# Context times Wo added to x as a step of its own, and a third key tile added on VectorE, in a fused attention, decoder and expert kernel

## The reference, cut to what matters

```
h   = x + relu(x @ w_down) @ w_up                 # w_down, w_up made from the condition
sim = cumulative products of path agreements      # from sigmoid(h @ Wp + bp), 8 heads, depth 5
ctx = softmax(causal sim) @ (h @ Wv)              # 8 heads of 32 numbers
x   = x + ctx @ Wo
U   = cond @ W_dec + b_dec                        # per batch: 257 rows of 30
z   = x @ U[:-1] + U[-1]                          # 30 numbers a token
y   = z @ V                                       # the decoder's output, 256 numbers
e   = argmax over 8 experts of y @ gate_w.T
out = x + y + y @ expert_w[e].T
```

## Time and profile before

| | |
|---|---|
| executions shown | 152.51, 152.74, 153.7 us; median 152.74 us |
| profiled execution | 153.3 us, of which the span is 151.2 us |
| TensorE (PE) busy | 141.7 us, 94% of the span |
| VectorE (DVE) busy | 87.6 us, 58% |
| ScalarE (ACT) busy | 56.4 us, 37% |
| GpSimd (POOL) busy | 30.2 us, 20% |
| chain of work that ended last | TensorE 84%, VectorE 11% |
| granted TensorE clock | 1.000 of full speed |

### The profile page before, as it was taken

How to read it: one execution, slowest core, us unless ns; L and a number is a source line. 1 busy time by engine, 2 the same in 40 slices (tenths; PEclk the granted TensorE clock), 3 DMA queues, 4 the chain that set the end, 5 groups by cost and what they waited for, 6 DMA issues and landing times.

```text
span 151.2 us, 5082 instructions
## 1 busy us (share of the span) xinstructions
PE 141.7 (94%) x2294; PEld 89.3 (59%) x2294; DVE 87.6 (58%) x164; ACT 56.4 (37%) x67; POOL 30.2 (20%) x56
## 2 busy tenths in 40 slices
PE   5999679999979979999999999999999999999993
PEld 5646346554645655657566756576567677666651
DVE  0473727866794848387816575549256852975431
ACT  3013370564253225357522461673234447310010
POOL 7200022011042120650112224200222440110000
PEclk9999999999999999999999999999999999999999
DMA  4999999700111000000000000000011010101111
GB/s 109 316 399 424 385 365 351 255 9 0 18 32 21 4 0 4 0 4 4 35 35 4 35 7 4 35 4 32 3 39 39 0 38 1 39 35 39 69 41 69
DMA packets 7381, 12.50 MB, mean 83 GB/s; under 512 B 1552, under 2 KB 5808, under 8 KB 7232
## 3 DMA queue, kind: packets, MB, share of 16 engines
q1 hardware_dynamic: 7120, 11.73, 21.9%
q0 software_dynamic: 96, 0.05, 0.9%
q10 hardware_dynamic: 144, 0.39, 0.6%
HBM read 9.95 MB, written 2.22 MB: 81 GB/s over the span
## 4 chain that ended last, share of the span: by engine, by line
PE 84%; DVE 11%; issue 2%; ACT 1%; POOL 0%; POOLq 0%; ACTq 0%; DVEq 0%
PE work L588 39%; PE c_ps L588 23%; PE s_ps L588 16%; PE work L767 3%; DVE rden L440 2%; PE work L707 2%; DVE h_t L473 1%; ACT prob L387 1%; DVE feat L578 1%; DVE u_w L514 1%; DVE phi_t L490 1%; PE work L759 1%; DVE w_up L466 1%; DVE x_t L566 1%; DVE q_bd L495 0%
## 5 line engine op out<-in xcount | busy, mean ns | idle before, releaser
L387 ACT ACTIVATE prob<-s_ps 128x1536 f32<-128x1536 f32 (+1 forms) x24 | 38.3, 1594 | 43.5 <-PE s_ps L588 43.4
L440 DVE RECIPROCAL rden<-c_ps 128x256 f32<-128x256 f32 x16 | 28.1, 1758 | 22.7 <-PE c_ps L588 22.7
L364 POOL TENSOR_SCALAR_AFFINE_SELECT prob<-prob 128x1024 f32<-128x1024 f32 x16 | 19.2, 1202 | 90.3 <-ACT prob L387 90.3
L588 PE MATMUL s_ps<-phi_t 32*128 32x256 f32 (+1 forms) x384 | 24.2, 365 | 1.1 <-DVE phi_t L490 0.6
L588 PE MATMUL c_ps<-prob,v_sb 128*32 128x256 f32 (+1 forms) x384 | 24.9, 346 | 0.0
L588 PEld LDWEIGHTS s_ps<-phi_t 32*128 32x128 f32 x384 | 17.4, 184 | 11.1 <-issue 8.5
L588 PE MATMUL work<-ctx_t,mix_sb 128*32 128x256 f32 x256 | 17.0, 381 | 0.4
L588 PE MATMUL work<-zo_t,gexp 128*32 128x256 f32 x256 | 16.9, 379 | 0.0
L588 PEld LDWEIGHTS c_ps<-prob,v_sb 128*32 128x32 f32 x384 | 11.6, 110 | 8.7 <-issue 1.7
L588 PE MATMUL c_ps<-prob,ones 128*32 128x256 f32 (+1 forms) x256 | 16.3, 326 | 0.0
L588 PE MATMUL work<-w_vl,h_t 128*32 128x296 f32 x208 | 14.8, 416 | 0.9 <-DVE pick L551 0.5
(11 more groups left out here) (96 smaller groups left out, 133.3 us busy)
## 6 DMA issues: line engine op xcount, KB each, us to landing
wdec<-in_W_dec SPq DMA_DIRECT2D x1, 3855.0 KB, 18.2
x_t<-in_x_tr SPq DMA_DIRECT2D x4, 512.0 KB, 8.7
ex_t<-in_expert_tr SPq DMA_DIRECT2D x1, 2048.0 KB, 25.2
out_x<-x_t SPq DMA_DIRECT2D x16, 128.0 KB, 1.7
mix_sb<-in_mix SPq DMA_DIRECT2D x1, 776.0 KB, 19.7
lift_sb<-in_lift ACTq DMA_DIRECT2D x1, 384.0 KB, 3.8
w_vl<-in_vl SPq DMA_DIRECT2D x1, 296.0 KB, 5.0
first_sb<-in_first SPq DMA_DIRECT2D x1, 144.0 KB, 3.4
```

The source lines that it names most:

```text
L364: nc.gpsimd.affine_select(out=tri, in_=tri, compare_op=ALU.is_ge, fill=0.0, base=0, pattern=[[0, HG], [0, 2], [1, P]], channel_multiplier= ...
L387: nc.scalar.activation(prob[:, p % 2, :, 0:width(p)], s_ps[:, :, 0:width(p)], ACT.Exp).then_inc(exped, 1)
L440: link(nc.vector.reciprocal(rden[:], c_ps[m % 2][:, CW:2 * CW]))
L588: return nc.tensor.matmul(o, w, r, start=start, stop=stop, skip_group_check=True)
```

## The change

There is a new step `mix`, four to a batch: context times Wo alone (8 matmuls where `out` had 16), which VectorE adds to x in place. `out` keeps the half with the expert's matrix, and VectorE adds that as before, so that 16 such additions become 32. `zT` waits for the four (in the last batch: two and two) `mix` steps and uses the new x alone, with half its matmuls; `WoU` and its copy are gone, and so is the transposed Wo in the load of the weights.

In the last pair of a long chunk, VectorE now adds key tile 2 into `tiles` as well, after the exponential and the mask; the ones of that tile go from TensorE, and the ones times `tiles` come last in the pair's matmuls. This holds for 7 of the 8 long chunks; the last pair of the kernel is left as it was. `add` thus stands ahead of 15 pairs instead of 8.

`zs` copies the scores to SBUF and releases its bank with that copy; the search for the best expert reads the copy, and a new count (`picked`) tells GpSimd of its end.

```diff
+def long(p):
+
+    return pair(p)[1][1] == 1 and p < ALL - 1
+
+
 def adds(p):
 
-    return sum(opening(i) for i in range(p + 1))
+    return sum(long(i) for i in range(p + 1))
...
-    elif n1 < B:
-        gaps[0] += [("WoU",)] if b == 1 else []
-        gaps[1] += [("zs", prv, ALL_T), ("zo", prv, 0), ("zo", prv, 1), ("VL", n1, 0), ("VL", n1, 1)]
-        gaps[2] += [("VL", n1, 2), ("VL", n1, 3)]
     else:
-        gaps[1] += [("zs", prv, ALL_T), ("zo", prv, 0), ("zo", prv, 1)]
-        gaps[4] += [("zs", b, FIRST), ("zo", b, 0)]
-    if prv >= 0:
-        gaps[3] += [("zoT", prv, 0), ("zoT", prv, 1)]
+        gaps[1] += [("mix", prv, 3)]
+        gaps[3] += [("zs", prv, ALL_T), ("zo", prv, 0), ("zo", prv, 1)]
+        gaps[4] = [("zoT", prv, 0), ("zoT", prv, 1)] + gaps[4]
+        if n1 < B:
+            gaps[1] += [("VL", n1, 0)]
+            gaps[2] += [("VL", n1, 2)]
+        else:
+            gaps[5] += [("zs", b, FIRST), ("zo", b, 0)]
...
-        gaps[3] += [("Q",), ("gup", n2)]
-        gaps[4] += [("G", 0), ("ubT",)]
+        gaps[3] += [("Q",), ("gup", n2), ("mix", b, 0)]
+        gaps[4] += [("G", 0), ("ubT",), ("mix", b, 1)]
         gaps[5] += [("G", 1), ("down", n2)]
     else:
-        gaps[0] += [("zT", prv, ALL_T)]
-        gaps[3] += [("out", prv, 0)]
-        gaps[4] += [("out", prv, 1)]
-        gaps[5] += [("out", prv, 2)]
+        gaps[0] += [("mix", prv, 2)]
+        gaps[2] += [("zT", prv, ALL_T)]
+        gaps[3] += [("mix", b, 0)]
+        gaps[4] += [("out", prv, 0), ("mix", b, 1)]
+        gaps[5] += [("out", prv, 1)]
+        if n2 < B:
+            gaps[5] += [("down", n2)]
+    if prv >= 1:
+        gaps[0] += [("out", prv - 1, 2)]
+        gaps[1] += [("out", prv - 1, 3)]
     if b >= 1 and n1 < B:
-        gaps[2] += features(n1, ALL_T)
-    if prv >= 1:
-        gaps[1] += [("out", prv - 1, 3)]
-    if b >= 1 and n2 < B:
-        gaps[5] += [("down", n2)]
+        gaps[1] += [("VL", n1, 1)]
+        gaps[2] += [("VL", n1, 3), *features(n1, ALL_T)]
     if b == B - 1:
-        gaps[2] += [("zT", b, FIRST)]
-        gaps[5] = [("zoT", b, 0), ("out", prv, 2), ("out", prv, 3)]
+        gaps[3] = [("mix", b, 0)]
+        gaps[4] = [("mix", b, 1), ("out", prv, 0), ("zT", b, FIRST)]
+        gaps[5] = [("out", prv, 1), ("zoT", b, 0), ("out", prv, 2)]
...
-        if _p + 1 < ALL and opening(_p + 1):
+        if _p + 1 < ALL and long(_p + 1):
             ORDER += [("add", _p + 1)]
-ORDER += [("zT", B - 1, SECOND), ("out", B - 1, 0), ("zs", B - 1, SECOND), ("zo", B - 1, 1),
-          ("out", B - 1, 1), ("zoT", B - 1, 1), ("out", B - 1, 2), ("out", B - 1, 3)]
...
+                    acc = tiles[:, chunk(p) % 2]
                     dve.wait_ge(exped, p + 1)
-                    nc.vector.tensor_tensor(tiles[:, chunk(p) % 2], both[:, :, 0, :], both[:, :, 1, :], ALU.add
-                                            ).then_inc(added, 1)
+                    if opening(p):
+                        nc.vector.tensor_tensor(acc, both[:, :, 0, :], both[:, :, 1, :], ALU.add).then_inc(added, 1)
+                    else:
+                        dve.wait_ge(masked, masks(p))
+                        dve.wait_ge(added, adds(p) - 1)
+                        nc.vector.tensor_tensor(acc, acc, both[:, :, 0, :], ALU.add).then_inc(added, 1)
...
+                    sc = score[:, span]
...
+                    nc.vector.tensor_copy(sc.rearrange("p t e -> p (t e)"), bank(s)[:, P:P + nt * E]
+                                          ).then_inc(empty(s), 1)
+                    done(dve, s)
                     link(nc.vector.reduce_max(smax[:, span], sc, AX_X))
...
-                if half and last:
-                    pe.wait_ge(added, adds(p))
-                    for h in range(HG):
-
-                        mm(c_ps[m % 2][DH * h:DH * (h + 1), CW:2 * CW], ones[:], tiles[:, m % 2, h, :],
-                           start=False, stop=False)
                 for i, (kt, q0, n) in enumerate(units):
                     lo = q0 % CW
                     for h in range(HG):
                         ins = mm(c_ps[m % 2][DH * h:DH * (h + 1), lo:lo + n],
                                  v_sb[:, b % 2, kt, DH * (HG * g + h):DH * (HG * g + h + 1)],
                                  prob[:, p % 2, h, CW * i:CW * i + n], start=(kt == 0), stop=(last and i == 1))
-                    if half and first:
+                    if half and (first or i == 0 and p < ALL - 1):
                         continue
                     for h in range(HG):
 
                         ins = mm(c_ps[m % 2][DH * h:DH * (h + 1), CW + lo:CW + lo + n], ones[:],
-                                 prob[:, p % 2, h, CW * i:CW * i + n], start=False, stop=(last and i == 1))
+                                 prob[:, p % 2, h, CW * i:CW * i + n], start=False, stop=(not half and i == 1))
+                if half and last:
+                    pe.wait_ge(added, adds(p))
+                    for h in range(HG):
+
+                        ins = mm(c_ps[m % 2][DH * h:DH * (h + 1), CW:2 * CW], ones[:], tiles[:, m % 2, h, :],
+                                 start=False, stop=True)
                 ins.then_inc(summed, 1)
...
-                elif kind == "WoU":
...
-                        done(pe, ("WoU",))
-                    pe.wait_ge(ctx_ready, BC * b + (NG if ts == FIRST else BC))
-                    for c in range(2 * DC):
+                        pe.wait_ge(u_ready, 1)
+                    for i in range(TT):
+                        if i // DC in (t // 2 for t in ts):
+                            done(pe, ("mix", b, i))
+                    for c in range(DC):
                         for t in ts:
-                            tok = slice(P * t, P * (t + 1))
-                            w = u_w[:, c, b, :] if c < DC else wo_u[:, c - DC, KP * b:KP * (b + 1)]
-                            r = x_t[:, b, c, tok] if c < DC else ctx_t[:, b % 2, c - DC, tok]
-                            ins = mm(o[KP * t:KP * (t + 1), 0:P], w, r, start=(c == 0), stop=(c == 2 * DC - 1))
+                            ins = mm(o[KP * t:KP * (t + 1), 0:P], u_w[:, c, b, :], x_t[:, b, c, P * t:P * (t + 1)],
+                                     start=(c == 0), stop=(c == DC - 1))
...
-                elif kind == "out":
+                elif kind in ("mix", "out"):
                     _, b, i = s
-                    if b == 0 and i == 0:
-                        done(pe, ("G", 0))
-                        done(pe, ("G", 1))
                     row, half = slice(P * (i % DC), P * (i % DC + 1)), slice(CW * (i // DC), CW * (i // DC + 1))
-                    for c in range(2 * DC):
-                        if c == DC:
-                            done(pe, ("zoT", b, i // DC))
-                        w = wo[:, c, row] if c < DC else gexp[:, c - DC, row]
-                        r = ctx_t[:, b % 2, c, half] if c < DC else zo_t[:, c - DC, half]
-                        ins = tiled(o[:, 0:CW], w, r, start=(c == 0), stop=(c == 2 * DC - 1))
+                    if kind == "mix":
+                        if b == 0 and i == 0:
+                            pe.wait_ge(ld_mix, 16)
+                        pe.wait_ge(ctx_ready, BC * b + NG * (i // DC + 1))
+                    else:
+                        if b == 0 and i == 0:
+                            done(pe, ("G", 0))
+                            done(pe, ("G", 1))
+                        done(pe, ("zoT", b, i // DC))
+                    for c in range(DC):
+                        w = wo[:, c, row] if kind == "mix" else gexp[:, c, row]
+                        r = ctx_t[:, b % 2, c, half] if kind == "mix" else zo_t[:, c, half]
+                        ins = tiled(o[:, 0:CW], w, r, start=(c == 0), stop=(c == DC - 1))
```

More of the change, by code:

```diff
@@ L247, in build @@
         kmax = sb("kmax", [P, TT])
+        score = sb("score", [P, TT, E])
         hit = sb("hit", [P, TT, E])
@@ L282, in build @@
         u_ready = sem("u_ready")
+        picked = sem("picked")
         zo_ready = sem("zo_ready")
@@ L806 @@
         "vl": halves(np.concatenate([a["attn_Wv"], a["attn_Wp"]], axis=1)),
-        "mix": np.concatenate([halves(a["attn_Wo"]), halves(a["attn_Wo"].T), v4, halves(v4.T),
+        "mix": np.concatenate([halves(a["attn_Wo"]), v4, halves(v4.T),
                                halves(a["ffn_gate_w"].T)], axis=1),
```

32 lines of the change are left out of this document (11 added, 21 removed).

## The result

| | before | after |
|---|---|---|
| executions, us | 152.51 to 153.8, median 153.22 | 161.51, 162.73, 163.4, median 162.73 |
| ratio | | 1.062 [1.057, 1.067]: slower |
| profiled execution, its span | 153.3, 151.2 | 162.73, 160.6 |
| mean granted clock of that execution | 1.000 | 0.979 |

The change costs 6.2%. The forecast, 159.2, had the side right and the size too small; 162.73 lies 0.23 us over the range and in the stretch that the prediction gave to the case "the clock falls".

What follows compares the result with a forecast made beforehand. TensorE was taken as the bound, but VectorE's in-order queue would make it wait: 4.0 for the laid order, 2.1 restarts and 0.4 mask make 6.5 us, giving 159.2 us against the median of 152.74; range 155.0 to 162.5.

Steps and rivals of the forecast that it cites:

- the clock falls: Rival: TensorE's clock drops to 1.2 GHz in the new waits, adding 3 to 6 us, 162 to 165; chance 0.06.
- Wait 1: Pairs 9 and 15: key-tile addition stands behind the features on VectorE, so TensorE waits 2.3 us before the ones times `tiles`.
- At the end, 0.5, 0.7, 1.7 and 1.3: Batch 3 and the end: forecast TensorE waits, in us, at zoT20, zoT21, out22 and zoT31.
- mix00's 1.6: Batch 0: mix00 needs the bank of `Q`, whose copies end late, so TensorE waits 1.6 us.
- the hand-laid order: New order laid end to end from 37.6 us with profiled step lengths; last addition to x at 152.65 against 148.64, +4.0.
- wait 2: Pairs 11 and 17: zoT soon after zs; TensorE waits 0.5 for GpSimd, 0.7 for mix10's bank, 0.2 at `phi21`.
- The stretched mask of pair 21: Batch 3: mask begins 0.45 before `add 20` ends and is stretched, and `add 21` waits for it: +0.4 us (0 to 0.8).
- the sum of 6.5: Whole forecast loss in us: 4.0 from the laid order, 2.1 from slow restarts, 0.4 from a stretched mask.
- about 10 lie on the path: +2.1: Of 24 new TensorE waits, about 10 on the path each bring a slow restart of 0.21: +2.1 us (0 to 5.0).

Runs made afterwards that it cites:

- e2: Changed kernel with the key-tile addition of pairs 9 and 15 put ahead of the features on VectorE: 159.41 us, 1.042 of the kernel before.
- e10: e1 plus the same four groups of unused matmuls ahead of mix00 in batch 0: 161.44 us, 1.055 of the kernel before.
- e1: Changed kernel with four groups of unused matmuls filling TensorE's waits in pairs 9 and 15: 161.08 us, 1.053 of the kernel before.
- e5: e2 with zT and zs each one gap earlier in batches 1 to 3: 162.95 us, 1.062 of the kernel before.
- e11: e2 with out21 ahead of the last context instead of behind it: 160.35 us, 1.040 of the kernel before.
- e3: Changed kernel with the third key tile alone undone; mixes, scores copy and new order stay: 159.53 us, 1.042 of the kernel before.
- e4: Kernel before, its order kept, with the third key tile alone added: 153.32 us, 1.001 of the kernel before.
- e9: e4 with the key-tile addition of pairs 3, 9 and 15 between the bias and the rest of the features: 150.88 us, 0.987 of the kernel before.
- e7: e5 with batch 0's mixes one gap later, then mix, zoT and out moved in all batches: 159.67 us, 1.046 of the kernel before.
- e8: e4 with the key-tile addition of pairs 3, 9 and 15 ahead of the features: 153.09 us, 1.001 of the kernel before.

## Why the prediction was right on the waits and wrong on the clock

**Right: VectorE's order, not its busy time.** TensorE lost work and the kernel lost time, since steps of VectorE came late. Wait 1 was 2.3 forecast and 1.99 and 1.98 measured, released by the named addition, and it goes when the addition is moved (e2). At the end, 0.5, 0.7, 1.7 and 1.3 forecast are 0.41, 0.52, 1.37 and 1.09; in batch 0, mix00's 1.6 is 1.43. All come out shorter by 0.1 to 0.3; at wait 1, 0.18 of it is that the record before it ends 0.40 behind its start (70.23), where the hand-laid order used the pitch, 0.22.

**Partly right: wait 2.** At zoT00 and zoT10 nothing was waited for in the kernel after: with mix10 and scores 11 at the low clock, zo had time to come. In its place `phi` waits 1.0 in each of the two batches for ScalarE's copies of zo_t, where 0.2 was forecast. With the clock full (e10) the forecast waits at zoT are there, 0.4 and 0.5. The stretched mask of pair 21 took 1.39, so 0.29 was lost where 0.4 was forecast.

**Wrong: the case "the clock falls in the new waits" got 0.06 and no place in the sum.** This is the step that failed: the sum of 6.5 had nothing for the clock, and in the traces it cost 2.5 us (1.25 and 1.28 behind the two waits 1); without them the profiled execution, 162.73, would have been at 160.2, in the range. It came true in all three executions counted (0.968 to 0.989). As a case it was priced higher, 3 to 6 us, for it came in two places and not in three batches; while steps ran slowly the waits for zo behind them vanished. TensorE's busy time, forecast to fall by 6 us, fell by 2.1, mostly for the same reason: slow steps count as busy (mix10 and scores 11 are some 1.6 us longer in each place). What the rows of before could not show, how the clock answers a wait of 2 us in a stream that is otherwise full, is what decided between 160 and 163, and a chance of 0.06 for it had no row behind it. The Trainium skill, TensorE: Matmul & The Clock Gate, section A second HAM failure mode: psum-queue depth-cycling, tells of a kernel that idles shortly but often as it cycles through banks and whose clock goes back and forth for it. The traces of after, e1, e5 and e11 agree that short waits can do it (0.66 to 0.90 in stretches of 5 us at and behind waits of 1.4 to 2.0), but here single waits in a full stream did it, not frequent ones.

**Mis-sized, and for another reason: "about 10 lie on the path: +2.1" for the restarts.** With the clock full the last mark lies 156.61 - 152.65 = 4.0 over the hand-laid order, of which 0.2 is e10's own filling; 2.5 was added for restarts and the mask, so 1.2 is missing. But the restart itself was misread. The 1.08 of `WoU` in the earlier trace rows runs to the end of its last record; in the timeline of before, the next step begins 0.90 behind its start, 0.03 more than a zT's 0.87:

```profile
54.38 1.08 PE L588 MATMUL work<-u_w,mix_sb 128*32 128x128 f32 x32 [0.77 <-DVE h_t L473]
55.28 0.62 PE L588 MATMUL c_ps<-prob,v_sb 128*32 128x256 f32 x8
```

The timeline of the kernel after shows the same: a `mix` behind a wait and one without, each ahead of scores, and a step of that size ahead of another of its kind:

```profile
41.88 1.07 PE L602 MATMUL work<-ctx_t,mix_sb 128*32 128x256 f32 x16 [1.43 <-DVE q_bd L505]
42.88 0.94 PE L602 MATMUL s_ps<-phi_t 32*128 32x256 f32 x16
...
51.83 1.05 PE L602 MATMUL work<-ex_t,mix_sb 128*32 128x256 f32 x16
52.69 1.05 PE L602 MATMUL work<-x_t,w_dn 128*32 128x256 f32 x16
...
57.44 1.05 PE L602 MATMUL work<-ctx_t,mix_sb 128*32 128x256 f32 x16
58.41 1.15 PE L602 MATMUL s_ps<-phi_t 32*128 32x256 f32 x16
```

From start to start: 1.00 behind the wait and 0.97 without, so a wait adds 0.03, not 0.21, and 24 of them make 0.7. What is longer is a step ahead of scores: 0.97 where one ahead of its own kind takes 0.86, and 0.86 is what the prediction took for mix10 ahead of scores 11 (wait 2). Behind 37.6 us there are 19 scores steps, so up to 19 x 0.11 = 2.1 us are missing from a laid order by this. That is an estimate, and no run takes it, or the restarts, away by itself: how the 3.7 us over the hand-laid order divide is open. The excess stands in every section (1.01 at the end of scores 8, 0.2 of it the filling, then a further 0.50, 0.71 and 1.74), which fits steps that are everywhere a little longer; at the end there is besides a wait of 0.77 for ScalarE's copies of zo_t, behind zoT31, that the prediction does not name.

**The balance.** Against its own profile I forecast 159.8; the profiled execution took 162.73 and began 0.84 early, so 163.57 by the shifted marks. Of the 3.8 between, 2.5 are the clock and 1.2 what is missing above.

**The parts.** In the new order the third key tile costs 3.2 us (162.73 against e3's 159.53), and putting its addition first in two places won 3.3 (e2), so most of it came through wait 1 and the clock; in the old order it costs nothing (e4) and in a better place it wins 1.9 (e9). The mixes with the new order cost 6.3 (e3). I tried other places for them (e5 to e7) and always found another step of VectorE late; whether some order carries 16 more additions to x with two banks for all such steps is open, these runs only show that none of the orders tried does.

## What to carry to other kernels

An engine that is a third idle can still be the one that is late: before work is moved to it, follow its queue at the place where the other engine next needs it, and look for a place just behind a short instruction that a third engine waits for (e8 against e9: the same addition, no gain or 1.3%). When a wait of a microsecond or two enters a stream of matmuls that had none, price the clock on its own, as a case with a real chance, and when an order is laid by hand, take the length of a step from start to start with the step that will follow it. Try the parts of a change alone and in the old order: here one part, in another place, was worth having.

## What the runs showed of the hardware

**The clock fell behind waits of 1.4 to 2.0 us, once behind two shorter ones, and not each time.** Behind 1.99 and 1.98 in the kernel after; behind 1.43 in e1's profiled execution and not in that of the kernel after, though the two programs are the same up to there; behind 1.47 in e11 and not behind 1.48 in e2; in e3 in the last step, behind two waits of 1.09 and 0.77 (0.80 from 150 to 155), where the kernel after and e10 kept it. In the kernel after, the timeline marks no wait of TensorE from 55.04 to the one at 72.62, and none from 78.61 to the one at 106.78. Each fall that could be read alone cost 1.25 to 1.35 us. Matmuls in the wait whose result nobody reads kept it at 2.4 GHz (e10): in pairs 9 and 15 two fillings of 1.73 (32 records), 3.5 us of useless work, gave back 2.5 us.

**VectorE and GpSimd lengthened each other** by more than I had allowed for: a VectorE instruction of 0.19 took 1.05 in e5, since it began 0.08 behind a mask's start and ended with it, and GpSimd's four products took 3.36 in place of 2.33 under VectorE's addition of a key tile and the bias behind it (0.74 in place of 0.32). The Trainium skill, SBUF — State Buffer, section Who interferes with whom, has this as a rule for a VectorE instruction with two inputs in SBUF beside a GpSimd one that reads it: the later is blocked, not slowed. The first of the two traces agrees to 0.03 us (68.59 against the mask's end at 68.56).
